# Attention's weights and its row of numbers 0 to 127, put into a PSUM bank and read from there

## The reference, cut to what matters

```python
h = jnp.einsum('nf,fhd->nhd', x, W)                       # 8 heads of 32
e = jax.nn.leaky_relu(a_src[src] + a_dst[dst], NEG_SLOPE)
e_max = jax.ops.segment_max(e, dst, num_segments=N)
e_exp = jnp.exp(e - e_max[dst])
denom = jax.ops.segment_sum(e_exp, dst, num_segments=N)
alpha = e_exp / (denom[dst] + 1e-16)
msg = h[src] * alpha[:, :, None]
out = jax.ops.segment_sum(msg, dst, num_segments=N)
```

## Time and profile before

| what | us |
| --- | --- |
| median of 3 runs | 3577.02 |
| lowest and highest run | 3572.45, 3579.33 |
| the profiled execution, its own time | 3579.75 |
| its span, first to last instruction | 3578.0 |
| GpSimd busy over the span | 1991.3 (56%) |
| VectorE busy over the span | 1708.5 (48%) |
| first and last start of attention's gathers (L604) | 119.1, 1194.4 |

### The profile page before, as it was taken

One profiled execution on the slowest core, in us unless ns is written; L12 is line 12 of the kernel. 1 busy time (PEld: TensorE's weight loads), 2 busy tenths in 40 slices (PEclk: granted clock), 3 DMA queues, 4 the chain that ended last, 5 costly groups with the idle time before them and its releaser, 6 DMA issues. The chain is left out here.

```text
span 3578.0 us, 49607 instructions
## 1 busy us (share of the span) xinstructions
PE 2507.4 (70%) x12468; PEld 1999.4 (56%) x12469; DVE 1708.5 (48%) x3583; ACT 974.1 (27%) x1944; POOL 1991.3 (56%) x2005
## 2 busy tenths in 40 slices
PE   5466555566655552999924888888888878639993
PEld 4344444444444352888824776777677754427772
DVE  5466666676666682111166444444444444621115
ACT  4300000000000031544443233333333324624441
POOL 0577777777777356222204777777777730463331
PEclk9687888787887755999967999999999989769996
DMA  5444444444444235222255555555555510242226
GB/s 154 123 129 130 127 128 129 129 133 132 128 127 128 70 110 204 81 78 83 77 188 164 155 156 158 157 157 158 158 157 152 157 54 2 94 162 83 88 89 245
DMA packets 319883, 459.13 MB, mean 128 GB/s; under 512 B 56729, under 2 KB 213962, under 8 KB 319498
## 3 DMA queue, kind: packets, MB, share of 16 engines
q0 software_dynamic: 94560, 261.75, 24.5%
q1 hardware_dynamic: 212888, 180.18, 16.9%
q10 hardware_dynamic: 12276, 15.62, 1.3%
HBM read 376.96 MB, written 80.39 MB: 128 GB/s over the span
## 5 line engine op out<-in xcount | busy, mean ns | idle before, releaser
L604 POOL DMA_INDIRECT room<-h_table,src_idx x784 | 837.7, 1068 | 354.4 <-issue 238.5
L2153 POOL DMA_INDIRECT em_msg<-xn_table,src_idx x784 | 746.8, 953 | 337.2 <-issue 238.5
L1105 PE MATMUL at_ps<-room,at_member 128*128 128x264 f32 x1584 | 495.3, 466 | 91.4 <-DVE room L961 88.7
L2229 PE MATMUL em_pse<-em_We,em_attr_t 128*128 128x256 f32 x1552 | 397.4, 414 | 158.3 <-DVE em_msg L2177 158.3
L2177 DVE TENSOR_TENSOR em_msg<-em_pse,em_msg 128x1024 f32<-128x1024 f32 x196 | 230.8, 1219 | 548.2 <-DMA em_msg<-xn_table,src_idx 548.2
L2229 PEld LDWEIGHTS em_pse<-em_We,em_attr_t 128*128 128x128 f32 x1552 | 312.5, 206 | 227.3 <-DVE em_msg L2177 169.0
L1105 PEld LDWEIGHTS at_ps<-room,at_member 128*128 128x128 f32 x1584 | 341.8, 227 | 173.6 <-DVE room L961 100.5
L2282 ACT ACTIVATE em_msg<-em_msg 128x1024 f32<-128x1024 f32 x196 | 207.2, 1057 | 682.5 <-DVE em_msg L2177 675.3
L2236 PE MATMUL em_psa<-em_msg,em_member 128*128 128x256 f32 x1584 | 359.7, 380 | 2.1 <-DVE acc L2187 2.1
L2236 PEld LDWEIGHTS em_psa<-em_msg,em_member 128*128 128x128 f32 x1584 | 302.1, 191 | 43.8 <-DVE acc L2187 2.5
L1785 POOL DMA_INDIRECT y_table<-room,m0e_dest x104 | 99.7, 958 | 298.3 <-DVE room L1805 292.9
(11 more groups left out here) (395 smaller groups left out, 3928.6 us busy)
## 6 DMA issues: line engine op xcount, KB each, us to landing
em_attr<-in_edge_attr_dram SPq DMA_DIRECT2D x97, 512.0 KB, 4.2
room<-x_sorted SPq DMA_DIRECT2D x105, 258.0 KB, 2.7
at_dst_row<-dst_flat SPq DMA_DIRECT2D x98, 256.0 KB, 3.8
room<-h_table,src_idx POOLq DMA_INDIRECT x784
at_resets<-reset_flat SPq DMA_DIRECT2D x784, 8.0 KB
em_msg<-xn_table,src_idx POOLq DMA_INDIRECT x784, 2.8
room<-in_x_dram SPq DMA_DIRECT2D x12, 896.0 KB, 10.3
cn_rows<-y_table SPq DMA_DIRECT2D x5, 1792.0 KB, 10.2
```

What stands on the lines that cost most here:

```text
L604: pool.indirect_dma_start(msg[:, s, j, :], None, mem.h_table[:, :], bass.IndirectOffsetOnAxis(ap=mem.src_idx[:, c:c + 1].bitcast(u32), axi ...
L1105: ins = nc.tensor.matmul(ps_a[:, which, 0:MSG], member[which][:, j, :], msg[:, s, c, :], start=(j == 0), stop=(j == CB - 1))
L2153: pool.indirect_dma_start(msg[:, s, j, :], None, mem.xn_table[:, :], bass.IndirectOffsetOnAxis(ap=mem.src_idx[:, c:c + 1].bitcast(u32), ax ...
L2229: ins = nc.tensor.matmul(ps_e[h][:, j, :], attr_t[:, s % 2, c * P:(c + 1) * P], We[:, :], start=True, stop=True)
```

## The change

The weights are now also written to a PSUM bank of their own, `ps_w`: 128 numbers per partition, chunk by head. The bank's next 128 columns hold the numbers 0 to 127, copied once from `iota_row`. The weighing takes its weights from there, and a mark of the first window takes its numbers from there. Because that bank is written by ScalarE and read by VectorE, a mark and a weighing wait for a new semaphore, `weight_out`. The weight columns in the rows are still written, since TensorE sums them too; it now waits for `weighted` itself, and so does `shift_scores` for that of the step before. The bank comes from `ps_a`, which keeps two; sums of further windows go to free columns of `ps_r`.

```diff
-        ps_a = ctx.enter_context(nc.psum_tensor("at_ps", [P, 3, 512], fp32))
+        ps_a = ctx.enter_context(nc.psum_tensor("at_ps", [P, 2, 512], fp32))
+        ps_w = ctx.enter_context(nc.psum_tensor("at_psw", [P, 512], fp32))
...
+        weight_out = sem("weight_out")
...
+        sums = [ps_a[:, 0, 0:MSG], ps_a[:, 1, 0:MSG], ps_r[:, HEADS:HEADS + MSG]]
+        weight_row = ps_w[:, 0:P]
...
-            dve.wait_ge(made, 2)
+            nc.vector.tensor_copy(ps_w[:, P:2 * P], mem.iota_row[:, :]).then_inc(made, 1)
+            dve.wait_ge(made, 3)
 
             def mark(dst, b, r):
-                return nc.vector.scalar_tensor_tensor(dst[:, :, :], mem.iota_row[:, :].unsqueeze(1).to_broadcast([P, CB, P]),
+                numbers = ps_w[:, P:2 * P] if isinstance(r, int) else mem.iota_row[:, :]
+                return nc.vector.scalar_tensor_tensor(dst[:, :, :], numbers.unsqueeze(1).to_broadcast([P, CB, P]),
                                                       col(mem.neg_base, r),
                                                       cols(mem.key_e, b * CB, CB).unsqueeze(2).to_broadcast([P, CB, P]),
                                                       op0=ALU.subtract, op1=ALU.is_equal)
...
             def shift_scores(k, s, i):
                 dve.wait_ge(turned_back, k + 1)
+                if not isinstance(k, int) or k > 0:
+                    dve.wait_ge(weighted, k)
...
                 b = 2 * k + p
                 dve.wait_ge(first_summed, b + 1)
+                dve.wait_ge(weight_out, k + 1)
                 mark(member[p], b, 0).then_inc(first_ready, 1)
...
-                nc.vector.scalar_tensor_tensor(tile_at(acc, t), ps_a[:, bank, 0:MSG], col(mem.in_first, b), tile_at(acc, t),
+                nc.vector.scalar_tensor_tensor(tile_at(acc, t), sums[bank], col(mem.in_first, b), tile_at(acc, t),
                                                op0=ALU.mult, op1=ALU.add)
...
             def weigh(k, s, quarter):
-                dve.wait_ge(weighted, k + 1)
+                dve.wait_ge(weight_out, k + 1)
                 part = msg[:, s, quarter * HC:(quarter + 1) * HC, :].rearrange("p c (h w) -> p (c h) w", w=HW)
+                of_part = weight_row[:, quarter * HC * HEADS:(quarter + 1) * HC * HEADS]
                 nc.vector.tensor_tensor(part[:, :, 0:HD], part[:, :, 0:HD],
-                                        part[:, :, HD:HW].to_broadcast([P, HC * HEADS, HD]), ALU.mult).then_inc(msg_done, 1)
+                                        of_part.unsqueeze(2).to_broadcast([P, HC * HEADS, HD]), ALU.mult).then_inc(msg_done, 1)
...
-            pe.wait_ge(made, 2)
+            pe.wait_ge(made, 3)
...
                     pe.wait_ge(first_out, 2 * k + p + 1)
+                    if p == 0:
+                        pe.wait_ge(weighted, k + 1)
...
             def weights(k, s):
                 act.wait_ge(shifted, 2 * k + 2)
+                nc.scalar.activation(weight_row.rearrange("p (c h) -> p h c", h=HEADS), shift[:, :, :], ACT.Exp).then_inc(weight_out, 1)
                 nc.scalar.activation(weight_col(s), shift[:, :, :], ACT.Exp).then_inc(weighted, 1)
```

More of the change, by code:

```diff
@@ L944, in add_rows @@
                 b = 2 * k + p
-                nc.vector.scalar_tensor_tensor(tile_at(acc, t), ps_a[:, bank, 0:MSG], col(mem.in_first, b), tile_at(acc, t),
+                nc.vector.scalar_tensor_tensor(tile_at(acc, t), sums[bank], col(mem.in_first, b), tile_at(acc, t),
                                                op0=ALU.mult, op1=ALU.add)
                 after = (t + 1).with_bounds(min_val=0, max_val=NA - 1)
-                return nc.vector.scalar_tensor_tensor(tile_at(acc, after), ps_a[:, bank, 0:MSG], col(mem.in_next, b),
+                return nc.vector.scalar_tensor_tensor(tile_at(acc, after), sums[bank], col(mem.in_next, b),
                                                       tile_at(acc, after), op0=ALU.mult, op1=ALU.add)
@@ L1104, in products @@
                     c = p * CB + j
-                    ins = nc.tensor.matmul(ps_a[:, which, 0:MSG], member[which][:, j, :], msg[:, s, c, :], start=(j == 0), stop=(j == CB - 1))
+                    ins = nc.tensor.matmul(sums[which], member[which][:, j, :], msg[:, s, c, :], start=(j == 0), stop=(j == CB - 1))
                 return ins
```

## The result

The changed kernel takes 3492.41 us (median of 4 runs, 3490.73 to 3494.79) against 3577.35 us (the kernel before, with a fourth run added to the three above): a ratio of 0.9765, 95% interval 0.9748 to 0.9782. The forecast was 3487 with a range of 3476 to 3512. The profiled execution took 3493.57 us, 86.2 less than the one of before (3579.75), where the sum said 90.

The account below looks back on a forecast made before the run. GpSimd's gathers at L604 were taken to set the attention stage's pace. From the profiled 3579.75 us, minus 96.0 of excess, plus 6 that stays, gave 3489.75; against the 3577.02 median, 3487 us, range 3476 to 3512.

Parts of the forecast that it names:

- the sum: Whole kernel: 96.0 us of gather excess removed, 6 us staying, from the profiled 3579.75 to 3489.75 us.
- What bounds: Attention stage: GpSimd's gathers at L604 set the pace, 21.95 us a step, and VectorE waits 4.9 us of it.
- What holds a gather: VectorE instructions with two SBUF tensors hold a gather about 0.13 us after its start; 96.0 us of excess.
- Excess that stays: Gathers at L604: +6 us remain from short VectorE instructions still taking two SBUF tensors; bounds nothing to 71 us.
- the four short instructions: L883, L886, L924 and L932 on VectorE, each step, still with two SBUF tensors; estimated at 5.5 us, taken as 6.
- Length of the six: Two marks and four weighings of a step: reading one operand from PSUM changes their own length by 0.
- the slower rival: VectorE becomes the bound because the marks and weighings lengthen reading PSUM; at twice the time 3699 us; chance 4%.
- The cover: VectorE in the new 20.1 us step: 3.05 us of waiting stay, so marks and weighings may grow 0.5 us each.
- ScalarE and the new waits: Attention step: second exponential, 49 x 0.44 us, runs when ScalarE is idle; new waits are met 8 us ahead.
- The destinations: SP queue's fetch at L822: spare time of 2.1 us a step shrinks to 0.3; about 2 us lateness costs nothing.
- The rule weighed against the change: Trainium skill's inferred addition: weighings, as tensor_tensor, would hold nothing, so their part of the excess would stay.
- Rival of one kind alone: Only marks freed: 32 us gone, 3545; or only weighings freed: 58 us gone, 3519; chance 4%.

Follow-up runs that it names:

- extra_psum: Changed kernel plus one unused VectorE product per step, one operand in PSUM and one in SBUF: 3488.59 us, 0.9761 of the kernel before.
- extra_sbuf: Changed kernel plus one unused VectorE product per step with both operands in SBUF: 3510.63 us, 0.9822 of the kernel before.
- sbuf_copy: Changed kernel with the new tile of weights and numbers in SBUF instead of PSUM: 3577.46 us, 0.9992 of the kernel before.
- extra_copy: Changed kernel plus one unused double-rate VectorE copy per step, SBUF to SBUF, 2048 numbers per partition: 3524.73 us, 0.9853 of the kernel before.
- marks_only: Changed kernel with the weighings reading their weights from SBUF again, only the marks reading PSUM: 3564.31 us, 0.9955 of the kernel before.
- extra_reduce: Changed kernel plus one unused single-rate VectorE sum per step over one SBUF tensor: 3491.31 us, 0.9758 of the kernel before.

## Why the prediction was right

*What bounds.* Right: extra_psum adds 1.2 us of VectorE work to every step and the time stays; extra_sbuf adds the same work with another operand and time follows the gathers.

*What holds a gather.* Right as far as this change goes, and shown by sbuf_copy: the place of one operand decides. The account was too narrow, though. It named two tensors from SBUF as the mark of a holder and one moment at which a gather can be held; extra_copy holds with one tensor, and at a second moment.

*Excess that stays.* 749.1 - 741.7 = 7.4 us, where 6 were taken from the four short instructions. The largest part comes from an instruction that was not among them, the destination mark (now L866), one SBUF tensor, 1024 numbers in 0.48 us (timeline of all engines, 553 to 556, of the kernel after):

```profile
554.28 0.48 DVE L866 TENSOR_SCALAR at_first_t<-at_dst_row,node_of 128x1024 bf16<-128x1024 int16 x1
...
554.38 1.20 POOL L604 DMA_INDIRECT room<-h_table,src_idx  x1 [0.30 <-issue]
```

554.38 + 1.20 = 555.58, again 0.82 behind the end of L866 at 554.76. Counted over the trace, L866 makes about 3.5 us of the excess, the four short instructions about 2.6 (they were given 5.5), and instructions ahead of the first step 1.3. So the term came out near its size by luck: what it was made of was mostly something else.

*Length of the six.* Right: 1206 and 1276 ns with an operand repeated out of PSUM, the form that no row of before showed. So the slower rival had no ground.

*The cover.* Mis-sized: 3.05 us was the idle time in front of the scores, and about 2.2 of it can be used. Nothing in this change needed it.

*ScalarE and the new waits.* Right that they are hidden: L857 and L971 stand idle for 0.7 and 0.0 us before their start, and no row names the exponential as their releaser. The one into PSUM takes 281 ns and not 440. The destinations are not late either: L866 waits 16.5 us for them, against 16.4 before, and SP's spare time is 29.8 us.

*The rule weighed against the change.* With the marks freed, weighings still hold gathers in marks_only, and freeing them is the larger part of the gain. The inferred addition in the Trainium skill, SBUF — State Buffer, section "Who interferes with whom", by which tensor_tensor does not stall DMAs because descriptor generation needs only the write side, disagrees with these runs, whose gathers read their index column in SBUF; the measurement decides.

*Rival of one kind alone.* It did not occur, but its prices were half wrong: 58 for the weighings held (62.5), 32 for the marks did not (19.1), because shares of holders that follow each other don't add. With the weighings freed, the marks are worth 775.2 - 749.1 = 26.1.

## What to carry to other kernels

When a GpSimd gather is the pace-maker, list the VectorE instructions that run when gathers are long, and compare ends: a constant distance (0.82 us here) from the end of an instruction is a hold, and a neighbour of equal length that holds nothing tells what to change. Putting one of two SBUF operands into PSUM freed the gathers here at no cost in VectorE's time; free all holders that stand behind each other, since one alone hands its gathers to the next. A wait of an engine is not all spare time: part of it can be time that the engine needs anyway.

## What the runs showed of the hardware

- A gather of 128 rows has two places at which VectorE can hold it. Two SBUF tensors hold it only near its start (0.82 us remain; 43 gathers in extra_sbuf). A copy at double rate holds it there (22 gathers in extra_copy) and near its end (0.12 us remain; 25 gathers).
- The hold does not depend on the number of inputs alone: one SBUF tensor at single rate (extra_reduce, 749.4 us of gathers) and PSUM with SBUF (748.6) hold nothing, one SBUF tensor copied at double rate (780.7) holds most. That the rate decides, and not the kind of instruction, is not shown: no run has a copy at single rate.
- ScalarE's exponential of 128 x 128 takes 281 ns into PSUM, 437 into an SBUF tile of the same layout (sbuf_copy), and 422 into the columns of the rows in SBUF.
